# Attention scores on four row groups of TensorE: a stack of 32 rows per head in place of one shared stack of 128

## The chip, the cores and the metric

The kernel runs on one core of one Trainium2 chip. The time is the device time of one execution in microseconds, the median of several runs; smaller is better. A second source is one execution taken by the hardware profiler, with its span and the start and end of every instruction.

## The reference

One transformer block over x of 4 batches, 512 tokens, 128 channels, in float32:

```
x = x + attention(layernorm(x));   x = x + ffn(layernorm(x))
attention: q, k, v = x @ w_attn + b_attn, 16 heads of 8 channels
  scores = q k^T / sqrt(8) + slope[head] * key position, causal mask
  y = softmax(scores) v, then @ w_proj + b_proj
ffn: gates = softmax(rmsnorm(x @ gate_w^T + gate_b) / 0.5), the best expert's gate g -> g/(g+1e-6)
  sum over 8 experts of gelu(x @ w1[e] + b1[e]) @ w2[e] + b2[e], times that gate
```

## The kernel before

The work is cut into 4 batches (b) of 4 sets (s) of 4 heads. The four heads of a set are called quads (q). Five engine programs are written out by hand and run against each other through semaphores; `n = 4*b + s` counts the 16 sets, and each set is walked in 16 places. `EARLY_PLAN` (n up to 4) and `LATER_PLAN` say at which place each piece of a set is issued; `STAGES` says where the side work goes (layernorm, projections, transposes, logits); `chunk`, `FFN1_AT` and `FFN2_AT` put 5, 1, 5 and 5 of the 16 FFN tiles of the batch behind into the sets s = 1, 2, 3 and the next 0.

Attention of one set has two score products. The first (`max_unit`, TensorE line 720, VectorE line 1047) makes scores with queries on the output partitions, and VectorE takes each row's causal maximum; it runs one set ahead. The maxima are transposed (L729), split into a high and a low part and copied by DMA into rows of the query stack (`load_max`, L385). The second (`exp_unit`, TensorE L742) makes scores with keys on the output partitions, the maximum already subtracted by those rows; a bf16 product adds the causal mask on the diagonal blocks (L748), and ScalarE takes the exponential out of PSUM (L553). `pv` multiplies it with the values (L767). Each product is 12 units a set: 3 kinds of causal blocks for 4 heads (one of 512 columns, one of 384 and 128, one of 256, so 16 products). Max units pass through three PSUM banks (`v_ring`, shared with all side work that VectorE takes out), exp units through three others (`a_ring`, shared with the FFN's first product, L673 to L675, which ScalarE takes out with Gelu at L570). The FFN's second product is L835.

To reach float32 accuracy q and k are split into high and low parts (`split_high` on ScalarE L594, `split_low` on GpSimd L442), and a score is the sum of three products of parts. Before, `q_stack` has two buffers of 128 rows: 32 rows of q_hi for the four heads, the same again, 32 rows of q_lo, and 32 constant rows (slopes, maxima). `k_stack` is one buffer with a slot for each quad; a slot holds k_hi, k_lo, k_hi in the 8 rows of its own head and zeros in the rows of the other three heads. So each product contracts all 128 rows. The stacks are filled by DMA from SBUF to SBUF. For a batch SyncE issues 3 copies of 256 KB for q (L366) and 16 of 32 KB for k_hi (L324), and GpSimd 8 of 32 KB for k_lo (L324). The k slots have one buffer, so the copies of its two halves wait until the sets that read them are done (`load_k`, `load_k_low`: half 0 at s = 2 of the batch ahead, half 1 at s = 0 of its own). SyncE runs its list in order; `load_max` of the next set stands behind these copies. `max_unit` of a batch waits at L712 for all of q, and at L715 for its own quad of k.

## Time and profile before

| | |
|---|---|
| three runs | 340.93, 341.5, 342.37 us, median 341.5 |
| span of the profiled execution | 341.4 us |
| PE, PEld busy | 295.9, 193.8 us |
| DVE, ACT, POOL busy | 192.6, 193.7, 84.1 us |
| chain that ended last | PE 74%, DVE 12%, DMA 7% |
| from 290.5 us on (FFN, no score product) | 50.9 us, PE busy 44.2 |

The page gives no time of the profiled execution other than its span; the median of the runs is 0.1 us above it. PE is TensorE's matmuls, PEld its weight loads, DVE VectorE, ACT ScalarE, POOL GpSimd; SPq is the queue of DMA issues on SyncE. A matmul's end is modelled, so from one matmul's start to the next one's start is the better measure of what it holds. PEclk 1.00 is 2.4 GHz and 0.50 is 1.2 GHz.

### The profile page before, as it was taken

The numbers are of one execution on the slowest core, as the hardware profiler recorded it, in microseconds if no ns is written. First come the engines' busy times: TensorE is split into PE (matmuls) and PEld (weight loads), VectorE is DVE, ScalarE is ACT, GpSimd is POOL, SyncE is SP. The second block draws the span as 40 slices with busy tenths as digits, with TensorE's granted clock in tenths as the row PEclk, the third lists the DMA queues.
The fourth block names the chain that finished last, engine by engine and source line by source line (L and its number), as shares of the span: only waits on it lengthen the run. The fifth ranks groups of instructions, "written<-read, shape, count | busy, mean of one in ns | idle before, by whom it ended". The sixth has DMA issues, their size and how long they took to land.

```text
span 341.4 us, 5507 instructions
## 1 busy us (share of the span) xinstructions
PE 295.9 (87%) x1784; PEld 193.8 (57%) x1784; DVE 192.6 (56%) x787; ACT 193.7 (57%) x322; POOL 84.1 (25%) x213
## 2 busy tenths in 40 slices
PE   0245899997979999699999997899999999998994
PEld 0133466565556676466766765557756665655661
DVE  5624759776786867145677776264867741161111
ACT  1871064463455568275759467376667788634462
POOL 8569203240233027002033126002210220000030
PEclk9985579999999999699999999899999999999999
DMA  7166500070120006200300028001100100000101
GB/s 198 66 90 96 193 2 2 16 122 9 38 74 4 0 19 105 29 2 18 95 1 4 0 61 120 3 2 44 35 4 2 35 2 2 0 2 0 31 1 31
DMA packets 12380, 13.29 MB, mean 39 GB/s; under 512 B 2048, under 2 KB 9088, under 8 KB 12096
## 3 DMA queue, kind: packets, MB, share of 16 engines
q1 hardware_dynamic: 11328, 11.90, 16.1%
q0 software_dynamic: 1024, 1.05, 1.9%
q8 instruction: 14, 0.23, 0.3%
q14 instruction: 14, 0.11, 0.1%
HBM read 5.21 MB, written 1.05 MB: 18 GB/s over the span
## 4 chain that ended last, share of the span: by engine, by line
PE 74%; DVE 12%; DMA 7%; issue 3%; ACT 1%; POOL 1%; DVEq 0%; SPq 0%; ACTq 0%; POOLq 0%
PE ffn_bank L835 16%; PE a_ring L742 11%; PE v_ring L720 11%; PE pv_bank L767 9%; DMA k_stack<-k_lo 6%; PE a_ring L673 5%; DVE unused L1047 5%; PE a_ring L748 5%; PE a_ring L674 4%; PE a_ring L675 4%; DVE xn L967 2%; PE v_ring L796 1%; PE v_ring L729 1%; DMA x_in<-x 1%; PE v_ring L673 1%
## 5 line engine op out<-in xcount | busy, mean ns | idle before, releaser
L1047 DVE CUSTOM_DVE_ANT_0 unused<-v_ring,cst 128x512 bf16<-128x512 f32 (+3 forms) x256 | 112.1, 487 | 68.5 <-PE v_ring L720 63.9
L553 ACT ACTIVATE probs<-a_ring 128x512 f32<-128x512 f32 (+1 forms) x192 | 92.5, 526 | 74.7 <-PE a_ring L748 73.5
L720 PE MATMUL v_ring<-k_stack,q_stack 128*128 128x512 f32 (+3 forms) x256 | 89.6, 422 | 20.2 <-DMA k_stack<-k_lo 15.3
L742 PE MATMUL a_ring<-q_stack,k_stack 128*128 128x512 f32 (+3 forms) x256 | 76.8, 360 | 0.4 <-DMA q_stack<-m_lo 0.4
L720 PEld LDWEIGHTS v_ring<-k_stack,q_stack 128*128 128x128 f32 x256 | 49.5, 210 | 40.6 <-issue 23.5
L570 ACT ACTIVATE hidden<-a_ring,cols_sb 128x512 f32<-128x512 f32 x64 | 43.4, 688 | 43.2 <-PE a_ring L675 42.7
L835 PE MATMUL ffn_bank<-hidden,w_sb 128*128 128x512 f32 x128 | 66.3, 602 | 1.1 <-ACT ffn_T L579 0.8
L742 PEld LDWEIGHTS a_ring<-q_stack,k_stack 128*128 128x128 f32 x256 | 46.7, 197 | 7.8 <-issue 4.0
L748 PE MATMUL a_ring<-score_mask,ident_bf 128*128 128x128 bf16 (+1 forms) x192 | 48.1, 252 | 0.0
L767 PE MATMUL pv_bank<-probs,v_ones 128*32 128x256 f32 (+3 forms) x512 | 43.2, 447 | 0.0
L673 PE MATMUL a_ring<-zT_hi,w_hi 128*128 128x512 f32 x64 | 34.2, 534 | 0.8 <-DVEq L953 0.8
L324 POOL DMA_DIRECT2D k_stack<-k_lo x32 | 18.1, 568 | 61.3 <-PE a_ring L748 60.5
L748 PEld LDWEIGHTS a_ring<-score_mask,ident_bf 128*128 128x128 bf16 x192 | 18.7, 98 | 20.6 <-issue 14.0
L674 PE MATMUL a_ring<-zT_lo,w_hi 128*128 128x512 f32 x64 | 26.1, 407 | 0.0
L675 PE MATMUL a_ring<-zT_hi,w_lo 128*128 128x512 f32 x64 | 25.9, 405 | 0.0
L835 PEld LDWEIGHTS ffn_bank<-hidden,w_sb 128*128 128x128 f32 x128 | 21.5, 192 | 5.9 <-ACT hidden L570 3.1
L1047 DVE DVE_READ_ACCUMULATOR2_ANT row_max<- 128x1 f32 x256 | 21.3, 83 | 0.0
L673 PEld LDWEIGHTS a_ring<-zT_hi,w_hi 128*128 128x128 f32 x64 | 12.7, 199 | 12.3 <-issue 7.9
L330 POOL TENSOR_SCALAR var<-mean_square 128x4 f32<-128x4 f32 x4 | 0.8, 193 | 73.8 <-DVE mean_square L1113 73.8
L767 PEld LDWEIGHTS pv_bank<-probs,v_ones 128*32 128x32 f32 x512 | 12.4, 110 | 10.0 <-issue 7.0
L570 ACT ACT_TABLE_LOAD x13 | 16.7, 1283 | 0.2
L674 PEld LDWEIGHTS a_ring<-zT_lo,w_hi 128*128 128x128 f32 x64 | 12.8, 200 | 5.0 <-issue 3.6
(109 smaller groups left out, 298.4 us busy)
## 6 DMA issues: line engine op xcount, KB each, us to landing
q_stack<-q_hi SPq DMA_DIRECT2D x8, 256.0 KB
k_stack<-k_hi SPq DMA_DIRECT2D x64, 32.0 KB
x_in<-x SPq DMA_DIRECT2D x4, 256.0 KB, 3.6
hidden<-w SPq DMA_DIRECT2D x1, 1024.0 KB, 8.3
q_stack<-q_lo SPq DMA_DIRECT2D x4, 256.0 KB
k_stack<-k_lo POOLq DMA_DIRECT2D x32, 32.0 KB, 4.0
w_sb<-w SPq DMA_DIRECT2D x1, 1024.0 KB, 5.2
x_res<-x SPq DMA_DIRECT2D x4, 256.0 KB, 3.1
```

What stands on the lines that cost most here:

```text
L324: queue.dma_start(k_stack[QR * g + q * D:QR * g + (q + 1) * D, 2 * half:2 * half + 2, q, :].bitcast(F32), part[rows:rows + QR // 2, :].bit ...
L553: act.activation(probs[:, n % 2, q, KIND_AT[kind]:KIND_AT[kind] + cols], a_bank()[:, 0:cols], ACT.Exp).then_inc(e_freed, 1)
L570: act.activation(hidden[:, n % HB, :], a_bank()[:], ACT.Gelu, bias=b1_cols[:, m:m + 1]).then_inc(g_freed, 1)
L673: pe.matmul(dst, lhs[0], rhs[0], start=True, stop=False)
L674: pe.matmul(dst, lhs[0], rhs[1], start=False, stop=False)
L675: return pe.matmul(dst, lhs[1], rhs[0], start=False, stop=True)
L720: last = pe.matmul(dst[:, at:at + P * (n + 1)], q_stack[b % 2][:, s, n * P:(n + 1) * P], k_stack[:, s, q, 0:P * (n + 1)], start=True, stop ...
L742: pe.matmul(dst[:, at:at + P * (TB - j)], k_stack[:, s, q, j * P:(j + 1) * P], q_stack[b % 2][:, s, j * P:T], start=(at == 0), stop=False, ...
L748: pe.matmul(diagonal, ident_bf[:], score_mask[:].unsqueeze(1).to_broadcast([P, blocks, P]), start=False, stop=True, skip_group_check=True) ...
L767: last = pe.matmul(pv_bank[QR * q:QR * (q + 1), j * P:T], v_ones[b % 2][:, j, s, q, :], probs[:, n % 2, q, at:at + cols], start=(s % 2 == ...
L835: pe.matmul(ffn_bank[:], w2_sb[:, m, :], hidden[:, n % HB, :], start=(m == 0), stop=(m == NT - 1)).then_inc(ffn2_done, 1)
L1047: ins = dve.tensor_tensor_reduce(unused[:, (uses[0] - 1) % V_BANKS, at:at + cols], bank_[:, at:at + cols], cst[:, C_MASK + T - cols:C_MASK ...
```

## The change

Each quad has 32 rows of its own in both stacks, 28 of them used: q_hi, q_lo, q_hi against k_hi, k_hi, k_lo (24 rows), two slope rows and two rows for the maximum. `k_stack` gets two buffers of the shape of `q_stack` and no zeros. A max product contracts 26 rows, an exp product 28, both from a start at row 32q. The copies become 12 of 64 KB for q and 12 for k in each batch, all issued by SyncE at s = 2 of the batch ahead, and for batch 0 the k copies are issued by ScalarE; the first max unit of a batch waits for all 24. The units of a set are ordered by kind and then quad, and issued in twos: at most places with scores, two exp masks come first, then two max products and two exp products whose quads are the other two.

```diff
 EARLY_PLAN = {
-    "max": (-1, 0, 2, 3, 4, 5, 6, 8, 8, 9, 11, 11), "take_max": (12,),
-    "exp": (4, 4, 5, 6, 8, 8, 9, 11, 11, 13, 14, 14), "pv": (11, 15), "pv_last": (0,),
+    "max": (0, 0, 2, 2, 4, 4, 6, 6, 8, 8, 10, 10), "take_max": (12,),
+    "exp": (4, 4, 6, 6, 8, 8, 10, 10, 13, 13, 15, 15), "pv": (11, 15), "pv_last": (1,),
 }
 LATER_PLAN = {
-    "max": (-1, -1, 2, 3, 4, 5, 6, 7, 8, 9, 10, 11), "take_max": (13,),
-    "exp": (4, 5, 6, 7, 8, 9, 10, 10, 12, 13, 14, 15), "pv": (12, 15), "pv_last": (0,),
+    "max": (-2, -2, 2, 2, 4, 4, 6, 6, 8, 8, 10, 10), "take_max": (12,),
+    "exp": (4, 4, 6, 6, 8, 8, 10, 10, 12, 12, 14, 14), "pv": (11, 15), "pv_last": (1,),
 }
...
-        k_stack = sb("k_stack", [P, SETS, QUADS, T], F32R)
+        k_stack = [sb(f"k_stack{i}", [P, SETS, T], F32R) for i in range(2)]
...
+        def send_term(queue, stack, term, part, loaded):
+            for q in range(QUADS):
+                row = QR * q + HEAD_D * term
+                queue.dma_start(stack[row:row + HEAD_D, :, :].bitcast(F32),
+                                part[QR * q:QR * (q + 1), :].bitcast(F32)).then_inc(loaded, 16)
+        def send_q(queue, b):
+            if b < 2:
+                queue.wait_ge(q_const, SETS * (b + 1))
+            else:
+                queue.wait_ge(e_filled, UNITS * SETS * (b - 1))
+            queue.wait_ge(q_split, 2 * b + 1)
+            send_term(queue, q_stack[b % 2], 0, q_hi, q_loaded)
+            send_term(queue, q_stack[b % 2], 2, q_hi, q_loaded)
+            queue.wait_ge(q_split, 2 * b + 2)
+            send_term(queue, q_stack[b % 2], 1, q_lo, q_loaded)
+        def send_k(queue, b):      # the same with k_hi to terms 0 and 1, k_lo to term 2, k_loaded
...
+        def exp_order(k):
+            return k // QUADS, (k + QUADS // 2) % QUADS
...
             def load_max(b, s):
                 sp.wait_ge(m_ready, SETS * b + s + 1)
-                for r, part in ((MAX_ROWS, m_hi), (MAX_ROWS + QUADS, m_lo)):
-                    sp.dma_start(q_stack[b % 2][r:r + QUADS, s, :].bitcast(F32),
+                for r, part in ((MAX_ROWS, m_hi), (MAX_ROWS + 1, m_lo)):
+                    sp.dma_start(q_stack[b % 2][r::QR, s, :].bitcast(F32),
...
-            load_q(0)
-            load_k(0, 0)
-            load_k(0, 1)
+            send_q(sp, 0)
...
                     if s == 0 and b >= 1:
-                        load_k(b, 1)
                         load_residual(b)
...
                     if s == 2 and b + 1 < B:
-                        load_k(b + 1, 0)
-                        load_q(b + 1)
+                        send_k(sp, b + 1)
+                        send_q(sp, b + 1)
                     if next_set(b, s)[0] < B:
                         load_max(*next_set(b, s))
...
-            pool.memset(k_stack[0:CONST_ROWS, 0:2, :, :].bitcast(F32), 0.0).then_inc(k_zeros, 1)
-            pool.memset(k_stack[0:CONST_ROWS, 2:4, :, :].bitcast(F32), 0.0).then_inc(k_zeros, 1)
-            load_k_low(0, 0)      # and the other calls of load_k_low, all on GpSimd
...
+            def k_constants(i):
+                for s in range(SETS):
+                    act.activation(k_stack[i][:, s, :], cst[:, C_KEY:C_KEY + T], ACT.Copy).then_inc(k_const, 1)
...
             split_high(0, 0)
+            send_k(act, 0)
             k_constants(1)
...
             def max_unit(b, s, k):
                 if k == 0:
-                    pe.wait_ge(q_loaded, q_count(b + 1))
+                    pe.wait_ge(q_loaded, STACK_LOADS * (b + 1))
+                    pe.wait_ge(k_loaded, STACK_LOADS * (b + 1))
+                kind, q = k // QUADS, k % QUADS
+                rows = slice(QR * q, QR * q + MAX_ROWS)
                 dst = v_bank()
                 at = 0
                 for n in MAX_BLOCKS[kind]:
-                    last = pe.matmul(dst[:, at:at + P * (n + 1)], q_stack[b % 2][:, s, n * P:(n + 1) * P],
-                                     k_stack[:, s, q, 0:P * (n + 1)], start=True, stop=True)
+                    last = pe.matmul(dst[:, at:at + P * (n + 1)], q_stack[b % 2][rows, s, n * P:(n + 1) * P],
+                                     k_stack[b % 2][rows, s, 0:P * (n + 1)], start=True, stop=True)
...
+            def exp_mask(b, s, k):
+                n = SETS * b + s
+                kind, q = exp_order(k)
+                dst = a_bank(e_freed, UNITS * n + k + 1)
                 blocks = len(KEY_BLOCKS[kind])
                 diagonal = dst[:].rearrange("p (a t) -> p a t", t=P)[:, 0::3, :][:, 0:blocks, :]
                 pe.matmul(diagonal, ident_bf[:], score_mask[:].unsqueeze(1).to_broadcast([P, blocks, P]),
-                          start=False, stop=True, skip_group_check=True).then_inc(e_filled, 1)
+                          start=True, stop=False, skip_group_check=True)
+                return dst
+            def exp_unit(b, s, k, dst):
...
+                rows = slice(QR * q, QR * q + STACK_ROWS)
+                at = 0
+                for j in KEY_BLOCKS[kind]:
+                    last = pe.matmul(dst[:, at:at + P * (TB - j)], k_stack[b % 2][rows, s, j * P:(j + 1) * P],
+                              q_stack[b % 2][rows, s, j * P:T], start=False, stop=True, skip_group_check=True)
+                    at += P * (TB - j)
+                last.then_inc(e_filled, 1)
...
                         side(b, s, k)
+                        if planned(b, s, k, "take_max") and next_set(b, s)[0] < B:
+                            transpose_max(*next_set(b, s))
+                        units = planned(b, s, k, "exp")
+                        masked = [exp_mask(b, s, unit) for unit in units]
                         for unit in maxima_due(SETS * b + s, k):
                             max_unit(*unit)
-                        if planned(b, s, k, "take_max") and next_set(b, s)[0] < B:
-                            transpose_max(*next_set(b, s))
-                        for unit in planned(b, s, k, "exp"):
-                            exp_unit(b, s, unit)
+                        for unit, dst in zip(units, masked):
+                            exp_unit(b, s, unit, dst)
```

## Rows read from the trace of the kernel before

**Rows 1.** The page: share of the span and instructions, engines in 40 slices, granted clock.
```profile
PE 295.9 (87%) x1784; PEld 193.8 (57%) x1784; DVE 192.6 (56%) x787; ACT 193.7 (57%) x322; POOL 84.1 (25%) x213
...
PEclk9985579999999999699999999899999999999999
```

**Rows 2.** Busy time of each engine in stretches that are one set each, clock, DMA.
```profile
38.60:50.70 12.10, 11.35 (x52) 7.42 (x51) 7.60 (x34) 5.64 (x12) 0.00 (x0) 0.65 0.10 31
50.70:63.75 13.05, 12.37 (x94) 8.03 (x93) 11.70 (x49) 5.50 (x13) 2.96 (x15) 1.00 0.00 1
...
177.30:197.10 19.80, 19.80 (x128) 13.62 (x126) 14.80 (x57) 12.91 (x21) 4.04 (x15) 1.00 0.01 2
```

**Rows 3.** The chain that ended last: two late stacks, one FFN product.
```profile
29.59 0.78 PE v_ring L720
...
147.87 0.86 PE ffn_bank L835 x2
...
214.57 1.19 PE v_ring L720 x3
```

**Rows 4.** TensorE in order of time: the two other late stacks, with its wait.
```profile
79.00 0.70 PE L720 MATMUL v_ring<-k_stack,q_stack 128*128 128x512 f32 x3 [2.77 <-issue]
...
139.70 1.19 PE L720 MATMUL v_ring<-k_stack,q_stack 128*128 128x512 f32 x3 [3.12 <-DMA k_stack<-k_lo]
```

**Rows 5.** TensorE in order of time, nine score units in a row (start, duration, line, tiles).
```profile
259.00 0.23 PE L748 MATMUL a_ring<-score_mask,ident_bf 128*128 128x128 bf16 x1
259.04 0.37 PE L720 MATMUL v_ring<-k_stack,q_stack 128*128 128x256 f32 x1
...
261.46 0.23 PE L748 MATMUL a_ring<-score_mask,ident_bf 128*128 128x128 bf16 x1
261.62 1.07 PE L767 MATMUL pv_bank<-probs,v_ones 128*32 128x512 f32 x8
```

**Rows 6.** Weight loads by shape: count, busy us, mean ns, idle before.
```profile
L742 PEld LDWEIGHTS a_ring<-q_stack,k_stack 128*128 128x128 f32 x256 | 46.7, 197 | 7.8 <-issue 4.0 <-ACT probs L553 3.0
...
L748 PEld LDWEIGHTS a_ring<-score_mask,ident_bf 128*128 128x128 bf16 x192 | 18.7, 98 | 20.6 <-issue 14.0
```

**Rows 7.** Weight loads in order of time: eight of the values' product.
```profile
251.76 0.16 PEld L767 LDWEIGHTS pv_bank<-probs,v_ones 128*32 128x32 f32 x8
```

**Rows 8.** VectorE in order of time: one head's maxima start to start.
```profile
66.50 0.69 DVE L1047 CUSTOM_DVE_ANT_0 unused<-v_ring,cst 128x512 bf16<-128x512 f32 x1 [0.66 <-DVE q_full L1011]
...
68.15 0.69 DVE L1047 CUSTOM_DVE_ANT_0 unused<-v_ring,cst 128x512 bf16<-128x512 f32 x1
```

**Rows 9.** SyncE's issues around the copies for batches 1, 2 and 3.
```profile
64.42 0.63 SPq L385 DMA_DIRECT2D q_stack<-m_lo  x1
65.15 5.69 SPq L324 DMA_DIRECT2D k_stack<-k_hi  x8
70.88 1.24 SPq L366 DMA_DIRECT2D q_stack<-q_hi  x2
...
121.56 0.63 SPq L385 DMA_DIRECT2D q_stack<-m_lo  x1
...
197.76 0.63 SPq L385 DMA_DIRECT2D q_stack<-m_lo  x1
```

**Rows 10.** A copy's way from issue to landing, in the chain.
```profile
39.26 1.91 DMA q_stack<-m_lo
```

**Rows 11.** Engines, clock, DMA share and GB/s: copies of q and k, then the half-speed stretch.
```profile
20.60:28.00 7.40, 0.08 (x1) 0.00 (x0) 0.88 (x4) 6.61 (x8) 6.66 (x10) 0.68 1.08 145
125.60:130.30 4.70, 4.70 (x27) 3.47 (x28) 3.53 (x19) 4.33 (x7) 2.00 (x7) 1.00 0.19 45
132.00:137.00 5.00, 4.58 (x46) 2.71 (x45) 3.21 (x14) 3.98 (x9) 4.37 (x9) 1.00 1.04 151
139.30:146.10 6.80, 6.40 (x21) 4.44 (x22) 1.39 (x6) 1.39 (x3) 0.00 (x0) 0.50 0.01 2
```

**Rows 12.** SyncE's DMA issues at the start: the first of q.
```profile
19.25 1.33 SPq L366 DMA_DIRECT2D q_stack<-q_hi  x2
```

More of the change, by code:

```diff
@@ L38 @@
 QR = P // QUADS
-TERMS = 3
 MASKED = -3.0e38
@@ L230, in block_kernel @@
         q_loaded = sem("q_loaded")
-        k_loaded = [[sem(f"k_loaded{half}{q}") for q in range(QUADS)] for half in range(2)]
-        k_low_loaded = [[sem(f"k_low_loaded{half}{q}") for q in range(QUADS)] for half in range(2)]
+        k_loaded = sem("k_loaded")
         m_loaded = sem("m_loaded")
@@ L433, in split_low @@
             def split_low(b, part):
-                full, hi, lo, parts, loads, count = (
-                    (k_full, k_hi, k_lo, k_split, k_low_loaded[0] + k_low_loaded[1], K_LOW_LOADS * b),
-                    (q_full, q_hi, q_lo, q_split, [q_loaded], q_count(b)))[part]
+                full, hi, lo, parts, loaded = ((k_full, k_hi, k_lo, k_split, k_loaded),
+                                               (q_full, q_hi, q_lo, q_split, q_loaded))[part]
                 pool.wait_ge(parts, 2 * b + 1)
                 if b >= 1:
-                    for loaded in loads:
-                        pool.wait_ge(loaded, count)
+                    pool.wait_ge(loaded, STACK_LOADS * b)
                 pool.tensor_tensor(lo[:], full[:], hi[:].bitcast(F32), ALU.subtract).then_inc(parts, 1)
@@ L447, in set_ones @@
                 pool.memset(slots[:, :, :, 16 + 8 * e:24 + 8 * e], 1.0).then_inc(v_const, 1)
-            def load_k_low(b, half):
-                if b == 0:
-                    pool.wait_ge(k_zeros, half + 1)
-                else:
-                    pool.wait_ge(e_filled, UNITS * (SETS * (b - 1) + 2 * half + 2))
-                pool.wait_ge(k_split, 2 * b + 2)
-                for q in range(QUADS):
-                    send_k(pool, k_lo, half, 1, q, k_low_loaded[half][q])
             steps = [0]
@@ L585, in split_high @@
             def split_high(b, part):
-                full, hi, ready, parts, loads, count = (
-                    (k_full, k_hi, k_ready, k_split, k_loaded[0] + k_loaded[1], K_LOADS * b),
-                    (q_full, q_hi, q_ready, q_split, [q_loaded], q_count(b)))[part]
+                full, hi, ready, parts, loaded = ((k_full, k_hi, k_ready, k_split, k_loaded),
+                                                  (q_full, q_hi, q_ready, q_split, q_loaded))[part]
                 act.wait_ge(ready, b + 1)
                 if b >= 1:
-                    for loaded in loads:
-                        act.wait_ge(loaded, count)
+                    act.wait_ge(loaded, STACK_LOADS * b)
                 act.activation(hi[:], full[:], ACT.Copy).then_inc(parts, 1)
@@ L1041, in max_unit @@
                 n = SETS * b + s
-                q, kind = k // KINDS, k % KINDS
+                kind, q = k // QUADS, k % QUADS
                 bank_ = v_bank()
```

110 lines of the change are left out of this document (35 added, 75 removed).

## The prediction, made before the result was known

> **What bounds the kernel now.** I read the page first: TensorE is busy 87% of the span and no other engine over 57% [rows 1], and the chain of waits is 74% TensorE. But an average over stages says little, so I cut the trace at the points where each set's maxima are sent, one stretch to a set. The reader should compare three numbers in each stretch: its length, PE's busy time and DVE's. A set with five FFN tiles lasts 19.80 us with PE busy for all of it, DVE 14.80 and ACT 12.91 [rows 2]; eight sets are filled like this (n = 5, 7, 8, 9, 11, 12 and with fewer tiles 13, 14). There TensorE is the bound and each microsecond off its list counts until DVE is met 5 us further down. The early sets have no FFN: 13.05 us with PE 12.37 and DVE 11.70 [rows 2]; a cut of TensorE's work brings about 1 us there. Third, the chain of waits in order of time shows where no engine bounds: at 79.0, 139.7 and 214.6 us TensorE starts the first maxima of a new batch after waits of 2.8 and 3.1 us for the stacks, and at 29.6 us for those of batch 0 [rows 3, 4]. Last, the tail from 290.5 us on has no score in it and doesn't move.
>
> **The score products.** Nine units (four max, five exp with their masks) take from 259.00 to 261.46, 0.27 us each, so the 24 of a set take 6.6 us when nothing holds them, and with the few waits at the edges 7.0 [rows 5]. The parts of that: a 128-column weight load is 0.20 us [rows 6], hidden behind the product before it and setting the pace of all but the 512-column ones, so 32 products are about 6.4 us, and 12 masks add 0.6. The change leaves the number of products, columns and weight loads as it is. All it can bring is that products of different row groups run beside each other. The trace of before has no row group, but it has column groups: the values' product runs as 128*32, its eight weight loads take 0.16 us together and its eight 512-column matmuls, two passes for each of four heads, 1.07 us [rows 5, 7], where one head's two passes alone would hold the array almost as long (the FFN's second product has the same two passes and takes 0.86 [rows 3]). So four column groups do overlap, loads too, nearly fully. I take the same for row groups.
>
> It isn't free. Going from 128*128 to 128*32 costs: the mask product starts at 261.46 and the next at 261.62, 0.16 us, where the mask in the middle of the run is followed after 0.04 [rows 5]. So about 0.11 us a switch. The change makes seven groups a set (places 2, 4, 6, 8, 10, 12 and the 14 that also holds the next maxima), each with a switch in and, before the masks or the side work, a switch back. A group: switch 0.11, a load that nothing hides 0.20, and the longest row group's stream, 0.21 for 512 columns or 0.19 + 0.05 where one quad has two products: 0.5 us. Six pairs of masks at switch 0.11 + load 0.10 [rows 6] + 0.12 of stream: 0.33 us. 7 x 0.5 + 6 x 0.33 = 5.5 us in place of 7.0. In the FFN sets the units before also wait here and there for a bank between other work, so that PE's list there holds more than 7.0; pairs need two of three banks at once and will wait in their own way. I take -1.8 us for each of the eight TensorE-bound sets: -14.4. Bounds: with no overlap the 6.4 us stay and 7 x 0.31 + 6 x 0.33 is added, 10.5 us, +3.5 a set; with a full fourfold overlap and the bank waits gone as well, -3.5 a set.
>
> For the early sets n = 0, 1, 3, 4 DVE is near: one head's four maxima hold it 1.65 us [rows 8], 6.6 a set, and its side work makes up the rest of 11.70. I take -1.0 each, -4.0, and -0.5 for the last set, where ScalarE has 12 exponentials to make. Sets n = 2, 6, 10 (s = 2) are in the next term.
>
> *A rule against the change.* The Trainium skill ("TensorEngine Tiling (Array Packing)", Key Properties) says that a change of tiling mode, unlike a change of tile, drains TensorE. The 0.16 against 0.04 us [rows 5] agrees; without that rule the set would come to 4.1 us by the terms above, with it to 5.5. The skill ("TensorE: Matmul & The Clock Gate", Measured speedup vs the span model) also gives 3.07 times for four products of 32 rows and 512 columns; by that, kind 0 alone, a group's 0.21 us of stream would be 0.28, and the set an estimated 6.0 us.
>
> **The stacks for the next batch.** Removed are the single k buffer's waits, eight issues on GpSimd and two memsets; none is on the path but for the first wait. Added is a longer list on SyncE: 24 copies at s = 2 in one piece, where 8 + 3 stood. SyncE pays 0.71 us for each 32 KB copy of k (5.69 for 8) and 0.62 for a 256 KB copy of q [rows 9], so the number of copies counts, not their bytes: 24 x 0.71 = 17.0 us, and 1.9 to the landing [rows 10], 18.9. The list can begin when the maxima of set 2 have been sent, at 65.05, 122.2 and 198.4 us [rows 9]. From there to the batch's first max product it took 13.9, 17.5 and 16.2 us before [rows 3, 4, 9], 47.6 together. After it takes 3 x 18.9 = 56.7: +9.1 us, whatever TensorE saves in sets 2. With sets 2 shorter by 1 to 2 us TensorE idles 6 to 9 us before each new batch. Behind the 24 issues stands `load_max` for set 3, which lands 1 to 2 us after the last stack copy; the exponentials of set 3 wait for it, but the first max units and the FFN products stand ahead of them. Bounds: 0.62 a copy gives 3 x 16.8, +2.8. On the other side the only rate of such copies is 45 GB/s, 32 KB at a time [rows 11], 1.4 us for 64 KB, which would be +59; but that rate is SyncE's pace of 0.71 us and no limit of the transfer, so I keep 0.8 us (+15.7) as the far end that I believe in.
>
> **The start.** Before, q is sent from 19.25 us and the first product runs at 29.59 [rows 3, 12]; it needed all of q and one quad of k's first half. After, it needs all 1.57 MB. Two queues issue 12 copies each: 19.25 + 12 x 0.71 + 1.9 = 29.7, no loss. By transfer: 1.57 MB at the 145 GB/s of that stretch [rows 11] is 10.8 us from 20.6, 31.4, with the landing 33.3: +3.7. At 92 GB/s, one 64 KB copy in 0.71 us, it is 39.6: +10. I take +3. ScalarE issues 12 copies (8.5 us) ahead of 8 constant copies; its first exponential waits for the maxima that are sent at 39.3 [rows 10], so they hide; without that cover it would be up to +8.
>
> **The clock.** After the 3.1 us wait before 139.7 the granted clock is 0.50, which is 1.2 GHz, for 6.8 us; the wait of 2.8 us before 79.0 left it at 1.00 [rows 1, 4, 11]. With three waits of 6 to 9 us I expect it to fall at all three: +1.5 us over the two falls of now.
>
> **Sum.** -14.4 - 4.0 - 0.5 + 9.1 + 3.0 + 1.5 = -5.3 on the span of 341.4: 336 us. The median of the runs stands 0.1 above that span, so the same holds for it: 336.
>
> **Rivals.**
> *Wide overlap.* The loads and streams of row groups overlap as the values' product does, and pairs don't wait for banks: -3 a set in eight, -1.5 in four, with +4.6 from the copies, 0 at the start and 1.5 for the clock: 341.4 - 24 - 6 + 6.1 = 317. For it: the 0.16 us for eight loads [rows 7], and that PE's time in the FFN sets is more than the sum of the dense rows. Against: DVE at 14.80 of 19.80.
> *No overlap (the other side).* If row groups load or stream one after another, each set has 10.5 us of scores in place of 7.0. It decides from the point where four loads of 0.20 us in a group go in a line: 32 x 0.20 is already the whole 6.4. 341.4 + 13 x 3.5 + 13.6 = 400 at worst, and with only +0.8 a set, where part overlaps, 365. For it: one weight path is all that the f32 rows show, each 128-column load at 0.20. Against: [rows 7].
> *The copies.* The transfers, not the issue, set the pace at 0.8 us or more: +15.7, and +7 at the start, in place of 9.1 and 3: 347. For it: k copies of 16 rows in the DMA share of 0.19 [rows 11], which could be few of the 16 engines working. By the Trainium skill ("DMA: Bandwidth & Descriptors", Why a DMA increments its semaphore by 16) a copy runs on the largest number up to 16 that divides both sides' outer sizes, here 8 engines of 16; the share of 0.19 at 45 GB/s doesn't settle it.
> *The clock.* TensorE does less in the same time, waits longer, and is granted 0.50 in the early sets as in the first [rows 2]: +2.5 in five sets and 3.4 after each of three waits: 336 + 20 = 356. For it: the set from 38.6 us has a mean of 0.65 with PE busy 11.35 of 12.10 by its rows. Against: the next has 1.00, and so has the page up to 136 us [rows 1, 2].
> *Nothing moves.* Waits for banks in pairs eat the gain: 341.
>
> **Chances.** Forecast 0.34 (own range 329 to 340), wide overlap 0.20, no or part overlap 0.14, copies 0.14, clock 0.12, nothing 0.06. A time within 0.5% (339.7 to 343.2) is what can't be told from no change. Faster: wide overlap, nine tenths of the forecast and a little of the others, 0.54; same 0.10; slower 0.36. Range 317 to 358, which leaves out most of the no-overlap case and the far half of the clock.
>
> **What would show it.** Row groups overlap if four 512-column products start within 0.1 us of each other and a group's next work begins 0.5 us after it; if their starts stand 0.2 us apart, they don't. SyncE's 24 issues should be one block of 16 to 17 us, and the first max products of batches 1 to 3 should start 19 us after the block's begin. FFN sets should be near 18.0 us with DVE at 14 to 15. The forecast is wrong if DMA landings trail the issues by more than 3 us, if PEclk is 5 in the slices past 50 us outside the three waits, or if DVE waits for TensorE less than now and the sets are longer.

## The result and the profile after

The changed kernel takes 409.64 us, median of 4 runs (407.19 to 415.06), against 341.94 (340.93 to 343.94) for the kernel before on the same chip: a ratio of 1.198, 95% interval 1.190 to 1.207. Where the runs of one kernel spread by more than 2%, the text gives their range, since a program's runs can fall into a faster and a slower state. 336 was forecast, in a range up to 358. The profiled execution has a span of 405.4 us and a mean granted clock of 0.81, where the one before had 341.4 and 0.95.

The page of the changed kernel, 40 slices of 10.1 us. Against [rows 1] TensorE is busy less of the time, and PEclk is 5 (1.2 GHz) through slices 3 to 12 but for one.

```profile
PE 314.5 (78%) x1784; PEld 165.6 (41%) x1784; DVE 187.5 (46%) x787; ACT 188.4 (46%) x322; POOL 58.7 (14%) x179
...
PE   0500588999798889847899898909999899898994
...
PEclk9955558555558599856999999557999999999999
```

Busy time by engine in stretches of the changed kernel: an early set, a set with five FFN tiles, the stretch of the first copies, and those in which the stacks of batches 1 and 3 are copied (columns as in [rows 2]: length, PE, PEld, DVE, ACT, POOL, clock, DMA share, GB/s).

```profile
99.50:116.85 17.35, 14.12 (x80) 5.93 (x77) 8.52 (x37) 5.05 (x11) 0.00 (x0) 0.50 0.11 18
...
292.00:311.10 19.10, 18.21 (x119) 9.84 (x118) 11.51 (x51) 12.12 (x20) 2.76 (x14) 1.00 0.06 15
...
24.00:41.00 17.00, 0.00 (x0) 0.00 (x0) 0.00 (x0) 4.63 (x8) 3.28 (x3) 0.50 0.96 112
82.00:104.00 22.00, 19.08 (x106) 8.63 (x105) 10.16 (x42) 7.45 (x16) 2.50 (x2) 0.50 0.47 74
...
246.00:273.00 27.00, 16.07 (x111) 7.56 (x109) 9.77 (x43) 11.31 (x18) 5.74 (x18) 0.66 0.50 62
```

Three things to see. The early set lasts 17.35 us at clock 0.50, where such sets had 1.00 and 13 to 14 us. The FFN set lasts 19.10 us at full clock, with PE idle 0.9 us and DVE at 11.5: it should have been 18.0. And while the copies for batches 1 to 3 run, the DMA share is 0.47 to 0.50. The stretch of the first copies has 0.96, but the 1 MB load of w2 runs in it too (0.68 in two_queues, which moves that load); from 18 to 22 us, where two queues send stack copies alone, it is 0.54 at 66 GB/s.

SyncE's issues at the end of batch 0's second set, as forecast one block of 17.7 us (81.73 to 99.47), where [rows 9] had 8 + 3 copies:

```profile
81.73 6.25 SPq L317 DMA_DIRECT2D k_stack<-k_hi  x8
88.03 2.81 SPq L317 DMA_DIRECT2D k_stack<-k_lo  x4
90.94 5.67 SPq L317 DMA_DIRECT2D q_stack<-q_hi  x8
96.66 2.81 SPq L317 DMA_DIRECT2D q_stack<-q_lo  x4
```

The chain of waits in order of time (start, length): from the last issue of each batch's copies to its landing, for batches 0 to 3. Compare 1.91 us in [rows 10].

```profile
23.64 17.01 DMA q_stack<-q_lo
...
98.80 5.47 DMA q_stack<-q_lo
...
176.36 8.57 DMA q_stack<-q_lo
...
262.60 10.97 DMA q_stack<-q_lo
```

TensorE's order of time in a full-clock set: masks, then two max and two exp units on four row groups, then side work.

```profile
211.06 0.28 PE L707 MATMUL a_ring<-score_mask,ident_bf 128*128 128x128 bf16 x2
211.27 0.45 PE L686 MATMUL v_ring<-k_stack,q_stack 26*128 26x384 f32 x2
211.28 0.50 PE L719 MATMUL a_ring<-q_stack,k_stack 28*128 28x512 f32 x2
211.56 0.22 PE L686 MATMUL v_ring<-k_stack,q_stack 26*128 26x128 f32 x2
211.71 0.66 PE L760 MATMUL v_ring<-cst,y_norm 128*128 128x128 f32 x4
```

All four units start within 0.02 us and the next work starts 0.44 us later: the row groups do run beside each other, weight loads too. So the change does what it says, and the time went elsewhere. One product more tells the clock without PEclk. The eight value products of 512 columns, which every set has once, take 1.06 or 1.07 us at 2.4 GHz [rows 5] and 1.94 at 1.2. In the kernel before none of the 16 sets has half-speed value products; in the changed kernel 7 have. This count is used below, because PEclk can be wrong: a run that comes next (quarter) has a set of 18 us with PEclk 1.00 and value products of 1.93 us.

```profile
257.04 1.94 PE L740 MATMUL pv_bank<-probs,v_ones 128*32 128x512 f32 x8
```
```profile
56.00:74.00 18.00, 16.39 (x99) 8.77 (x99) 12.27 (x46) 6.18 (x13) 2.88 (x9) 1.00 0.00 1
```
```profile
66.43 1.93 PE L740 MATMUL pv_bank<-probs,v_ones 128*32 128x512 f32 x8
```

### The profile page after: what moved, and what is told of

Read it like the earlier page. It is cut to its first block, busy times and chain, and to the rows that moved or that the text cites. A ratio compares the mean times of both kernels' runs of the same rounds, so it can differ in the third digit from the quotient of the medians.

```text
span 405.4 us, 5418 instructions
## 1 busy us (share of the span) xinstructions
PE 314.5 (78%) x1784; PEld 165.6 (41%) x1784; DVE 187.5 (46%) x787; ACT 188.4 (46%) x322; POOL 58.7 (14%) x179
## 3 DMA queue, kind: packets, MB, share of 16 engines
HBM read 5.20 MB, written 1.05 MB: 15 GB/s over the span
## 4 chain that ended last, share of the span: by engine, by line
PE 49%; DVE 14%; SPq 12%; DMA 11%; issue 6%; ACT 6%; POOL 1%; DVEq 0%; POOLq 0%; ACTq 0%
SPq L317 11%; PE ffn_bank L808 11%; DMA q_stack<-q_lo 10%; PE pv_bank L740 8%; PE v_ring L686 7%; DVE unused L1022 6%; PE a_ring L644 5%; PE a_ring L646 4%; PE a_ring L645 4%; PE a_ring L719 3%; PE a_ring L707 3%; ACT probs L527 3%; ACT L527 2%; DVE stats L933 1%; DVE z L942 1%
## 5 line engine op out<-in xcount | busy, mean ns | idle before, releaser
L527 ACT ACTIVATE probs<-a_ring 128x512 f32<-128x512 f32 (+1 forms) x192 | 90.5, 523 | 113.6 <-PE a_ring L719 113.3
L686 PE MATMUL v_ring<-k_stack,q_stack 26*128 26x384 f32 (+3 forms) x256 | 59.8, 451 | 48.3 <-issue 26.9
L808 PE MATMUL ffn_bank<-hidden,w_sb 128*128 128x512 f32 x128 | 68.4, 619 | 1.2 <-ACT ffn_T L553 0.8
L686 PEld LDWEIGHTS v_ring<-k_stack,q_stack 26*128 26x128 f32 x256 | 30.6, 218 | 72.0 <-issue 37.5
L740 PE MATMUL pv_bank<-probs,v_ones 128*32 128x256 f32 (+3 forms) x512 | 57.7, 557 | 0.0
L707 PE MATMUL a_ring<-score_mask,ident_bf 128*128 128x128 bf16 (+1 forms) x192 | 40.6, 269 | 18.1 <-ACT probs L527 18.1
L719 PE MATMUL a_ring<-q_stack,k_stack 28*128 28x512 f32 (+3 forms) x256 | 51.3, 441 | 0.0
L644 PE MATMUL a_ring<-zT_hi,w_hi 128*128 128x512 f32 x64 | 36.2, 566 | 3.0 <-DVEq L928 3.0
L351 POOL TENSOR_SCALAR var<-mv 128x4 f32<-128x4 f32 x6 | 1.2, 193 | 188.0 <-DVE mv L936 188.0
L719 PEld LDWEIGHTS a_ring<-q_stack,k_stack 28*128 28x128 f32 x256 | 25.6, 219 | 4.2 <-issue 2.8
L740 PEld LDWEIGHTS pv_bank<-probs,v_ones 128*32 128x32 f32 x512 | 13.4, 124 | 26.2 <-issue 19.6
L644 PEld LDWEIGHTS a_ring<-zT_hi,w_hi 128*128 128x128 f32 x64 | 12.9, 202 | 16.5 <-issue 10.1
```

Source lines behind the costliest of these rows:

```text
L527: act.activation(probs[:, n % 2, q, KIND_AT[kind]:KIND_AT[kind] + cols], a_bank()[:, 0:cols], ACT.Exp).then_inc(e_freed, 1)
L644: pe.matmul(dst, lhs[0], rhs[0], start=True, stop=False)
L686: last = pe.matmul(dst[:, at:at + P * (n + 1)], q_stack[b % 2][rows, s, n * P:(n + 1) * P], k_stack[b % 2][rows, s, 0:P * (n + 1)], start= ...
L707: pe.matmul(diagonal, ident_bf[:], score_mask[:].unsqueeze(1).to_broadcast([P, blocks, P]), start=True, stop=False, skip_group_check=True)
L719: last = pe.matmul(dst[:, at:at + P * (TB - j)], k_stack[b % 2][rows, s, j * P:(j + 1) * P], q_stack[b % 2][rows, s, j * P:T], start=False ...
L740: last = pe.matmul(pv_bank[QR * q:QR * (q + 1), j * P:T], v_ones[b % 2][:, j, s, q, :], probs[:, n % 2, q, at:at + cols], start=(s % 2 == ...
```

## The experiments

Each kernel was timed in 3 rounds (early_before in 5) beside the kernel before. All times are medians.

### What the copies cost

**quarter.** All 96 copies and their waits stay, with a quarter of the bytes.
```
- dma_start(stack[row:row + 8, :, :],   part[QR * q:QR * (q + 1), :])
+ dma_start(stack[row:row + 8, 0:1, :], part[QR * q:QR * q + 8, :])
```


> The changed kernel with the same 96 stack copies, their queues and their waits, but each carries 8 rows of 2 KB (16 KB, one set's) in place of 32 (64 KB): sets 1 to 3 of q and k are left out of the stacks. Theory A (the transfers of the 64 KB copies, not their issue, make most of the loss): SyncE's block of 24 issues stays at 17 to 18 us, the last landing trails it by 2 to 3 us instead of 5 to 11; the first maxima start at 30 to 31 us instead of 43.8 (-13) and the three waits shrink by about 5 us each (-15); with shorter waits TensorE spends less than 110 us at half clock instead of 154, and the time is 365 to 375 us. Rival B (the clock: packed score products leave TensorE too little to do and it stays at half clock in the early sets whatever the copies do): half clock still over 130 us and the time 381 us or more. Rival C (pairs of units waiting for two of three banks make most of the loss): the time falls by less than 20 us, to 390 or more.

374.7 us, 35 less than the changed kernel. The last landing now trails its issue by 1.95 us (batch 1) and 2.25 (batch 0), with SyncE's block still 16.3 us long. Theory A holds for the bytes; 374.7 is still 33 above the kernel before. Its part on the clock does not hold: with shorter waits 8 of 16 sets still have half-speed value products (profiled run, 383.3 us), against 7. That much of rival B is right.

**one_copy.** One copy to each stack and batch, 22 left out.
```
- for q in range(QUADS):      # in send_term
+ for q in range(1):          # and only the low term of q and of k is sent
```


> The changed kernel with one 64 KB copy to each of q's and k's stacks per batch (the low term of one head group) in place of 12; the other 22 are left out, and what is waited for is that one copy. Neither issue nor transfer of copies is left, so what stands above 341.5 us here is clock and banks. Theory A: first maxima at 27 to 29 us, the three batch intervals at the 14 to 16 us of the kernel before or less, half clock under 60 us in all, and 340 to 352 us; the sets in between gain nothing, since pairs wait for banks as much as they save. Rival B: half clock over 100 us, 365 us or more. The overlap as I forecast it (1.8 us less in each of eight sets): 325 to 330 us.

363.6 us, but the four runs spread from 354.9 to 371.0 at granted clocks of 0.84 to 0.92; the profiled one took 365.5. Issuing 22 more copies costs 11 us between the medians and 18 between the fastest runs of each, and their bytes 35 either way: 46 to 52 of the 68. Neither theory alone fits: the batch waits are gone, but 6 of 16 sets still have half-speed value products.

**wide_copies.** Two of three copies write 16 rows of two sets, the same 64 KB.
```
+ if term < 2: dst = stack[QR * q:QR * q + 16, 2 * term:2 * term + 2, :]
```


> The changed kernel with two of the three term copies of each head group shaped as 16 rows of two sets in place of 8 rows of four: the same 64 KB, the same count, queues and source rows, but 16 destination rows (the stacks hold displaced data). Theory A1 (a copy runs on as many of the 16 DMA engines as its rows divide into, 8 for the changed kernel's): the window of the copies moves 110 to 150 GB/s at a DMA share near 0.8 to 1 while these go, the last landing trails SyncE's last issue by 2 to 4 us instead of 5 to 11, the first maxima start at 36 to 40 us and the time is 375 to 392. Rival A2 (the rate is one of 2 KB rows within SBUF, whichever engines): 70 GB/s and landings as before, 405 to 412 us.

389.4 us, 20 less. Busy time in the stretches of copies of this kernel:

```profile
21.00:33.00 12.00, 0.00 (x0) 0.00 (x0) 0.00 (x0) 4.63 (x8) 5.95 (x4) 0.50 0.91 149
79.00:97.00 18.00, 11.51 (x71) 5.28 (x71) 7.75 (x37) 6.26 (x13) 2.50 (x2) 0.63 0.49 83
154.00:171.00 17.00, 11.48 (x89) 5.85 (x89) 8.05 (x38) 10.61 (x17) 5.77 (x18) 0.85 0.42 87
```

149 GB/s in place of 112 at the start (w2's load is in both) and 83 to 87 in place of 62 to 74 later, where a 64 KB issue in 0.71 us allows 92. The last landings of batches 1 to 3 trail by 4.1, 3.4 and 4.3 us in place of 5.5, 8.6 and 11.0, and at the start by 7.4 in place of 17.0. So the number of rows counts, as A1 says, though a third of the copies still has 8. A1's rates came only at the start; later the issues, one in 0.6 to 0.7 us, come too slowly for them. The Trainium skill ("DMA: Bandwidth & Descriptors", Why a DMA increments its semaphore by 16) says that a copy runs on the largest number of engines up to 16 that divides the outer sizes of both sides, here 8. The share of 0.47 to 0.50 with copies queued all the time agrees.

**two_queues.** k's copies for batches 1 to 3 on GpSimd's queue, w_proj and w2 loaded later.
```
- send_k(sp, b + 1)
+ send_k(pool, b + 1)
```


> The changed kernel, all its data in place, with k's 12 copies for batches 1 to 3 issued by GpSimd instead of SyncE, and the loads of w_proj and w2 behind the first maxima instead of between q's copies and them. If the second queue uses the DMA engines that the first leaves idle: SyncE's block falls from 17.7 to 8.6 us, the batch intervals from 25 to 16 to 18 us, and 409 becomes 375 to 390. If both queues end on the same half of the engines: the intervals stay at 22 us or more, only the start gains 3 to 5 us, 395 to 407.

408.3 us: no gain, and 1 us outside the second range. The 24 copies of batch 1 are issued in 8.5 us in place of 17.7, yet the first max product starts 22.1 us after the first issue, where the changed kernel takes 22.6. While both queues send, the DMA share rises, the bytes hardly (two stretches of 4 us of this kernel):

```profile
90.00:94.00 4.00, 3.08 (x18) 1.88 (x16) 3.38 (x17) 1.81 (x4) 4.00 (x8) 0.50 1.10 81
94.00:98.00 4.00, 3.64 (x23) 1.46 (x23) 2.23 (x12) 2.54 (x5) 2.02 (x3) 0.50 1.04 90
```

The changed kernel moves 74 and 88 GB/s there at a share of 0.55 and 0.53. So the transfers of copies with 8 rows set the pace, with one queue or two. Whether the second queue's packets ran on other engines or waited at the same ones is not shown.

**early_after.** The changed kernel, complete, with x, k and q of the next batch made one set earlier, k's copies sent in set 1, and FFN tiles spread evenly.
```
- "x_norm": (1, 7, -1), "x": (1, 10, -1), "k": (1, 12, -1), "q": (1, 15, -1)
+ "x_norm": (0, 7, -1), "x": (0, 10, -1), "k": (0, 12, -1), "q": (0, 15, -1)
- TILES = (5, 1, 5, 5)
+ TILES = (5, 4, 4, 3)
```


> The changed kernel, complete, with the next batch's x, k and q made one set earlier (in set 0 in place of set 1), k's copies issued in set 1 and q's in set 2, and the FFN tiles spread 5, 4, 4, 3 over the sets in place of 5, 1, 5, 5. Theory A: the copies end before the set that needs them, so the three waits (intervals of 22.6, 25.8 and 27.6 us) fall to 16 to 20 us, minus 18 to 25 us, and with 4 FFN tiles in the third set the clock stays at 2.4 GHz in batches 1 and 2; only the start (+14), the early sets' clock and the order's 12 us remain: 375 to 388. If the loss sits in the sets themselves: 395 or more. The load of the maxima for set 2 goes behind 12 of the copies on SyncE, which may give up to 3 us a batch back.

386.8 us, inside the expected range, 23 less than the changed kernel. TensorE's list of waits no longer has the stacks of batches 1 to 3, which in the changed kernel stood at 19.6 us (first fence, changed kernel; second, this one):

```profile
PE v_ring L686 <- issue: 26.9, 1, 26.9
PE v_ring L686 <- DMA q_stack<-q_lo: 19.6, 3, 10.0
```
```profile
PE v_ring L688 <- issue: 27.3, 1, 27.3
PE a_ring L709 <- ACT probs L529: 15.9, 29, 1.1
```

**early_before.** The same move in the kernel before, q's copies alone in set 1.

> The kernel before, complete, with the next batch's x, k and q made in set 0 in place of set 1, q's copies issued in set 1, k's as before in set 2, and the FFN tiles spread 5, 4, 4, 3 in place of 5, 1, 5, 5. The kernel before waits 2.8 to 3.1 us for the stacks at two batches and about as long for the third, and at two of them the granted clock falls for 3 to 7 us. With three copies fewer in the third set's list and k ready when the list begins, the first maxima of a batch should start 8 to 10 us after the list's begin in place of 13.9, 17.5 and 16.2: the waits go, minus 5 to 8 us, 333 to 337 us. If the side work moved to set 0 makes DVE or TensorE late there (sets with 5 tiles are full), the gain is eaten: 340 to 345 us.

347.3 us, 1.021 (1.015 to 1.028) of the kernel before: slower by about 2%. The wait for the stacks fell from 15.3 to 8.2 us, but the side work moved to set 0 made TensorE wait 4.9 us for z (1.4 before) and 7.8 for the banks of maxima (2.6). No complete version beats the kernel before.

### Order or layout

**order_old_layout.** Only the plan and order, on the old 128-row stacks (`k_stack[:, s, q, ...]` in place of `k_stack[b % 2][rows, s, ...]`).

> The kernel before with its stacks of 128 rows and its copies, and only the new plan and order: pairs of units, masks first, kind by kind, the transpose of the maxima ahead. No row groups, so no overlap is to be had. Theory A: start and batch waits as before (29.6 us; 13.9, 17.5, 16.2 us), clock as before; only the bank waits of pairs are added, 1 to 2 us a set in the ten sets with FFN tiles: 350 to 362 us. Rival C: pairs cost 3 us a set or more, 375 us and up. If the order costs nothing: 340 to 344 us.

353.8 us, ratio 1.040 (1.033 to 1.047), clock 0.965: the order alone costs 12 us.

**pairs_mask_last.** As that, with each mask behind its products again.

> The kernel of the new order on the old stacks, but with each unit's mask behind its products as before: pairs, kinds and places stay new. If the masks ahead (a pair's second mask waits for a bank while products could run) make the 12 us of the new order, this takes 341 to 345 us. If the pairs and places themselves do, 350 to 355 us. I expect 348: both.

359.2 us: slower still. So the masks ahead save 5 us and the pairs and their places cost 17. My 348 was wrong.

**layout_old_order.** Row groups and copies with the old plan, mask last.

> The changed kernel's stacks, row groups and copies, with the plan and the order of issue of the kernel before: single units, a head's three max kinds in a row, the mask behind its unit's products, the transpose of the maxima behind the max units. Theory A (copies): start and batch waits as in the changed kernel, first maxima at 43 to 45 us and batch intervals of 23 to 28 us; 395 to 412 us, so order is worth at most 15 us. Rival C (pairs and masks first cost the bank waits): at least 20 us back, 390 us or less. If instead the order is what lets row groups overlap, this is slower than 412 us.

445.4 us (two runs at 438, two at 453), slower than 412: the expectation's last sentence, not my theory. Its full-clock set with five FFN tiles lasts 21.10 us with PE busy throughout, against 19.10. That each single mask is now a switch and that single units rarely meet another row group is my reading; no run takes the two apart. The order costs 12 us without row groups and saves 31 to 36 with them.

### What the overlap is worth, and the clock

**rows_128 and one_group.** The one_copy kernel with only the rows changed that the score products read (and, in rows_128, the exponentials' input scaled down).
```
- rows = slice(QR * q, QR * q + MAX_ROWS)   # and STACK_ROWS for exp
+ rows = slice(0, P)                        # rows_128
+ rows = slice(0, MAX_ROWS)                 # one_group
```


> The one_copy kernel with each score product over all 128 rows of the new stacks in place of one head's 26 or 28 (a sum over four heads; the exponentials' input is scaled down to stay finite). Same instructions, order, copies and waits, but nothing can overlap. Theory R (products of few rows let the clock fall): granted clock near full but for the start, sets as in the kernel with the new order and the old stacks (19.2 us with five FFN tiles, 11.5 to 14.5 early), 340 to 352 us, so faster than the 363.6 of the version that overlaps. Rival (the clock falls because this order makes TensorE wait): the clock is as low as one_copy's 0.85 and the time is above 370.

> The one_copy kernel with all units reading the first head's rows (0 to 25 or 27), so that products are small and can't overlap. Theory R: what counts is the rows in use, so the clock is as low as in one_copy or lower (0.80 to 0.86), TensorE works longer at it, and the time is 375 to 400 us. Rival I (the clock falls because overlapped products leave TensorE less work in a set): here TensorE has as much work as with 128 rows and the clock stays above 0.92, 345 to 360 us.

347.6 us (clock 0.96 to 0.99) and 455.3 us (clock 0.73 to 0.87), against 363.6 (354.9 to 371.0) with four row groups. Half-speed value products: none in rows_128, in 13 of 16 sets of one_group. The PEclk lines below show too few for one_group: two of those sets lie in its first seven slices. PEclk of rows_128, then of one_group, and a stretch of one_group in which TensorE is idle for 0.1 of 19.4 us:

```profile
PEclk9999999999989999999999999999999999999998
```
```profile
PE 417.1 (93%) x1784; PEld 236.6 (52%) x1784; DVE 190.5 (42%) x787; ACT 190.3 (42%) x322; POOL 58.9 (13%) x179
...
PEclk9999999555558985755998595577997575789999
```
```profile
92.00:111.40 19.40, 19.31 (x81) 10.25 (x77) 7.67 (x34) 5.76 (x12) 0.00 (x0) 0.50 0.04 12
```

The rival said that the clock falls because overlap leaves TensorE less to do. In one_group it has more to do and the clock is lower still, so theory R holds on the clock: here, TensorE kept 2.4 GHz through products of 128 rows and lost it through products of 26 and 28. One_group's 455.3 us are far outside the 375 to 400 that R gave. The complete kernels agree: with the new order on 128 rows (order_old_layout) no set has half-speed value products, in the changed kernel 7.

The same set (n = 12, the first of batch 3, five FFN tiles) at full clock, in the kernel before, rows_128, one_group and one_copy:

```profile
231.80:250.90 19.10, 19.10 (x125) 12.93 (x124) 11.90 (x50) 12.37 (x21) 4.97 (x18) 1.00 0.14 36
```
```profile
228.70:247.90 19.20, 19.07 (x120) 12.39 (x119) 11.50 (x51) 12.19 (x20) 2.78 (x14) 1.00 0.05 15
```
```profile
311.70:332.70 21.00, 21.00 (x119) 12.31 (x118) 11.63 (x51) 12.19 (x20) 2.78 (x14) 1.00 0.05 14
```
```profile
250.20:269.30 19.10, 18.21 (x120) 9.85 (x118) 11.51 (x51) 12.11 (x20) 2.78 (x14) 1.00 0.05 15
```

Few rows without overlap cost 1.8 us (by my reading switches, and loads that nothing hides); overlap gives 1.9 back; in this set the sum is nothing. TensorE's own work did shrink, from 19.07 to 18.21 us, but the set did not. Over a longer piece at full clock it counts. From the sending of the maxima of n = 12 to the end no copies of stacks are awaited and all value products take 1.07 us. Kernel before, order_old_layout, rows_128, one_copy, changed kernel:

```profile
231.70:341.40 109.70, 102.98 (x577) 65.19 (x575) 44.68 (x185) 66.38 (x106) 12.70 (x51) 1.00 0.05 15
```
```profile
234.90:350.90 116.00, 105.44 (x577) 65.00 (x575) 44.93 (x190) 66.31 (x107) 12.69 (x51) 1.00 0.05 14
```
```profile
228.30:344.40 116.10, 105.52 (x578) 65.00 (x575) 44.96 (x190) 66.51 (x107) 10.54 (x47) 0.99 0.04 11
```
```profile
249.50:363.60 114.10, 101.92 (x578) 56.31 (x576) 44.87 (x190) 66.33 (x108) 10.57 (x47) 0.99 0.04 11
```
```profile
291.30:405.40 114.10, 101.85 (x578) 56.30 (x576) 44.90 (x190) 66.30 (x107) 10.47 (x47) 1.00 0.04 11
```

The new order adds 6.3 us here and the row groups take 2.0 back: with the clock held and the copies out of the way, the changed kernel is still 4.4 us behind. In one_group the same four units that took 0.44 us take 1.24 (320.23 to 321.47):

```profile
320.23 0.79 PE L682 MATMUL v_ring<-k_stack,q_stack 26*128 26x384 f32 x4
320.86 0.67 PE L715 MATMUL a_ring<-q_stack,k_stack 28*128 28x512 f32 x2
321.47 0.66 PE L756 MATMUL v_ring<-cst,y_norm 128*128 128x128 f32 x4
```

That is 2.8 times. The Trainium skill ("TensorE: Matmul & The Clock Gate", Measured speedup vs the span model) gives 3.07 for four products of 32 rows and 512 columns; the trace is near it. Two early sets, the same work in both kernels, in rows_128 and then in one_copy:

```profile
45.60:60.10 14.50, 13.38 (x103) 8.78 (x99) 12.12 (x46) 6.19 (x13) 4.07 (x15) 1.00 0.01 2
60.10:72.00 11.90, 10.80 (x86) 6.52 (x82) 8.52 (x38) 6.91 (x14) 2.53 (x2) 1.00 0.04 14
```
```profile
50.00:68.60 18.60, 16.99 (x104) 9.13 (x101) 12.28 (x46) 6.18 (x13) 3.03 (x10) 0.60 0.00 2
68.60:82.70 14.10, 12.46 (x85) 5.73 (x81) 8.32 (x37) 6.89 (x14) 2.50 (x2) 0.73 0.03 12
```

At a clock of 0.60 and 0.73 they take 6.3 us more, though overlap should have saved some. From the sending of the first set's maxima to that of the sixth's it is 63.7 us in rows_128 and 77.2 in one_copy: 13.5 of the 19.2 us between the two profiled executions lie in the five sets in which the clock fell most.

**fill_one_copy and fill_after.** Idle products of 128 rows and 512 columns, two ahead of each max pair in the sets with few FFN tiles, more where stacks are awaited.
```
+ pe.matmul(dst[:], ident_bf[:], score_mask[:] over 4 blocks, start=True, stop=True)
```


> The one_copy kernel (one stack copy to each stack and batch, the rest left out) with idle products added on TensorE: bf16, 128 rows, 512 columns, written into the bank that the next max product then starts afresh; two ahead of each max pair in the sets with no FFN tile or one (n = 0 to 4, 6, 10), 6 to 8 where a batch's first maxima wait. Theory B (the granted clock: packed score products with few FFN tiles around them let it fall to 1.2 GHz, which holds the eight 512-column value products at 0.88 us instead of 0.47): the value products are back at 0.47 us from about 60 us on, the early sets shorten from 14 to 18 us to 12 to 15, and 363.6 becomes 345 to 353, the time of the kernel with the new order and the old stacks. If the clock has another reason, the added 12 products of 0.22 us a set only add: 370 to 385 us.

> The changed kernel with the same idle products, 36 ahead of the first max product and 28 ahead of each later batch's. Theory B with A: the copies still arrive at the same times (first maxima at 44 us, batch intervals of 20 to 25 us), but sets run at 2.4 GHz in between, and 409 becomes 380 to 395. If the clock is only a consequence of waits that the copies would hide anyway, 400 to 412.

364.6 and 408.6 us: no gain beyond one_copy's own spread, though sets with half-speed value products fell from 6 to 1 and from 7 to 4. The set of one_copy that took 18.60 us takes 16.00 at clock 1.00, with 12 idle products (by estimate 2.6 us, at 0.22 each) in it. The four sets from there take 56.2 us in place of 61.9, and 50.9 in rows_128. The clock could be held, and it was worth 5.7 us there, but no gain in the whole time shows. Both branches of fill_one_copy's expectation failed; fill_after fell in its second, 400 to 412.

```profile
55.10:71.10 16.00, 14.25 (x114) 7.37 (x113) 12.29 (x46) 6.31 (x14) 3.55 (x13) 1.00 0.02 6
```

### Masks and banks

**one_copy_no_mask, before_no_mask, no_mask_fill.** The mask products are left out (`start=(at == 0)` on the first product instead, and the exponentials' input scaled by 1/64).

> The one_copy kernel without the 192 mask products (and with the exponentials' input scaled by 1/64 so that unmasked scores stay finite); units are still issued in pairs and in the same order. In a full-clock set of the one_copy kernel the masks hold TensorE 2.25 us (six pairs, each with a switch from row groups to 128 rows and back, and 0.64 us in a wait for a bank), where the single masks of the kernel before took 1.07. Theory M (the masks' switches ate what the overlap saved): sets with five FFN tiles shorten from 19.1 to 17.0 to 17.6 us, and 363.6 becomes 335 to 345. Rival (the chain of banks through ScalarE sets the pace of pairs): the sets stay within 0.6 us of 19.1 and the time is 355 or more. The clock may fall further with less work on TensorE, which would add up to 8 us to either.

> The kernel before, without its 192 mask products (exponentials' input scaled by 1/64), as the control. Its masks take 1.07 us in a full-clock set of 19.1 and need no switch: sets of 18.0 to 18.3 us, and 341 becomes 326 to 334. If this kernel gains as much as one_copy does without masks, the masks' cost is not one of row groups.

> The one_copy kernel without masks, with the idle products of 128 rows of fill_one_copy. With the clock held, a set with five FFN tiles, which has no idle product, should show what overlap without mask switches is worth: 16.8 to 17.6 us in place of 19.1; early sets of 11 to 13 us. In all 335 to 350 us. If the clock is still below 0.9, idle products in the sets with few FFN tiles aren't enough, and the time stays near the 366 of the version without masks.

366.6, 333.0 and 379.7 us. The control gains 8 us as expected; its full-clock set lasts 18.60 us in place of 19.10. The row-group kernel gains nothing from losing its masks, at a clock of 0.81 in three of four runs. (The fourth, the profiled one, took 388.2 at 0.68, so its trace is not compared.) In no_mask_fill the idle products did not hold the clock: the mean is 0.87, and 9 of 16 sets have value products of 1.4 to 1.9 us. Why it is 13 us slower than without them stays open. But its full-clock set of the table above lasts 18.80 us, where theory M gave 17.0 to 17.6, and there M fell. The chain of waits there does not run through TensorE but through VectorE's side work, with GpSimd's root of the variance between the two lines shown (14 steps of 0.2 us are left out):

```profile
273.56 0.89 DVE stats L937 x4
...
278.93 0.60 DVE z L946 x2
```

**a4.** Four banks for exponentials and FFN, two for maxima (`V_BANKS, A_BANKS = 2, 4` on one_copy).

> The one_copy kernel with four banks for exponentials and FFN tiles and two for maxima, in place of three and three. If pairs lose time because the second mask waits for a third bank of the exponentials (0.64 us in a set, 18 us in all by the waits), the full-clock sets shorten by 0.5 to 1 us and 363.6 becomes 350 to 358; the maxima with two banks may take that back: a pair then waits for VectorE's last of the pair before, 0.5 to 1.0 us for each of six pairs, which would be 370 to 385. Under theory M alone: no gain.

389.3 us, 26 more than one_copy and above the 370 to 385 expected. The masks' wait for ScalarE (18.0 us in one_copy) is gone, and about 20 us of waits for VectorE's maxima (1.1 in one_copy) take its place; 8 sets have half-speed value products in place of 6. So these pairs want more than two banks on the side of the maxima too.

## Why the prediction was wrong

The medians form a ladder: 341.9 before; 353.8 with the new order alone (+12); 347.6 with it, the new stacks, 128-row products and one copy (6 us back, which I read as the copies and their waits; no run takes them apart); 363.6 with row groups (+16 between medians, +9 between the fastest runs); 374.7 with all copies issued (+11, or +18); 409.6 with their bytes (+35).

**The copies: right on the issue, wrong on the transfer; the largest error.** This is the step of the prediction that failed. "The number of copies counts, not their bytes" was read from q's 256 KB copies [rows 9], and a batch was priced at 24 issues of 0.71 us and 1.9 us to the landing, 18.9. The block of 17.7 us came as worked out; then 5.5, 8.6 and 11.0 us to the landing stood in place of 1.9, and 17.0 at the start. From the list's begin to a batch's first max product it took 22.6, 25.8 and 27.5 us, 28 more than before in place of the 9.1 forecast, and the first max product of all ran at 43.8 us in place of 29.6, 14 later in place of 3. I had 1.4 us for a 64 KB copy (+59) in hand and laid it aside because SyncE's pace explained the row of 45 GB/s, and took 0.8 as the far end. At 62 to 74 GB/s a copy takes 0.9 to 1.05 us, between the two. 12.1 us were forecast for copies and start; they cost 42.5 by the trace, 46 to 52 by the experiments.

**The scores: the group was right, the sum was not.** A group of 0.5 us was forecast and is 0.44; row groups overlap. But -1.8 a set came out as 0.0 in the set of 19.10 us, and as -2.0 in all from n = 12 to the end, where -5.9 was forecast (three of the eight sets, and the last). TensorE's work in the FFN set fell by 0.9, half of what was forecast. I had charged the switches (1.43 us) to the new list and compared it with 7.0, while the dense rows that I quoted give 6.6, and left out the second mask's bank wait (18.1 us over the run). The rest is a limit that I had put too far away. "Each microsecond off its list counts until DVE is met 5 us further down" does not hold: with 1.6 us less on TensorE (no_mask_fill) the set still lasts 18.8, because the side work's chain through DVE and POOL ends last, which DVE's 14.80 us of busy time [rows 2] don't show.

**The clock: +1.5 forecast, +9 to +16 measured in the step to row groups.** The rival had the mechanism (early sets at half clock) and about the size, 20 us, but its reason, waits, was not needed. Without long waits 6 of 16 sets ran at half clock, and with 128-row products in the same places none. Its sum was also off: 2.5 in five sets and 3.4 after three waits, less the 1.5 already counted, is 21. The step also holds what overlap gives back, so the clock alone probably cost more than the step shows.

**The order** was costed at nothing beside its products. It is 12 us on the old stacks, 6.3 of it from n = 12 to the end.

**The rivals** were each priced alone. Copies (347) and clock (356) both came true, and no case added them. "No overlap", which carried the far side, did not occur. The size of the miss is partly chance: copies, order, clock and the missing gain each added.

What I had listed as signs against me were the right ones: landings more than 3 us behind the issues, and PEclk 5 past 50 us.

## What to carry over

For a copy within SBUF, count the rows on both sides before its bytes: at 8 rows, 64 KB took 0.9 to 1.05 us, at 16 it nearly kept up with an issue every 0.71. In these runs products of few rows let TensorE's clock fall, for the full-width work around them too, whether they overlapped or not; measure the full-clock set and the granted clock apart, and check PEclk against a product that every set has. When a list on the busiest engine is cut, follow the chain of side work in the same set first, since here its length and not its busy share was the floor.

## What the runs showed that I had not expected

TensorE at 93% busy with products of 26 rows was granted 0.73 to 0.87 of its clock, and at 128 rows, with the same instructions, 0.96 to 0.99. A second, software queue for copies of 8 rows raised the DMA share to 1.04 to 1.10 and hardly the bytes moved (81 to 90 GB/s against 74 to 88). Products of 26 rows that can't overlap are slower than those of 128 in the same order: 21.00 against 19.20 us a set.
